# GpSimd adds the exponentials of a head pair in two additions, one for each head

## What is computed

```python
h = _layernorm(x) * (1 + ca) + sa
q, k, v = split(einsum('bse,ehd->bshd', h, w_qkv))        # 16 heads of 64
logits = einsum('bqhd,bkhd->bhqk', q, k) / sqrt(64)        # causal mask
probs = softmax(logits, axis=-1)
x = x + ga * einsum('bshd,hde->bse', einsum('bhqk,bkhd->bqhd', probs, v), w_out)
```

## Time and profile before

| | |
|---|---|
| runs | 2799.43 us median of 3 (2799.24 to 2804.2) |
| profiled execution | 2801.26 us; its span from first to last instruction 2799.5 us |
| TensorE busy | 79% of the span |
| VectorE busy | 58% |
| ScalarE busy | 46% |
| GpSimd busy | 29% (804.5 us) |
| mean granted clock of TensorE | 0.905 of full speed |

### The profile page before, as it was taken

One profiled execution on the slowest core, in us unless ns is written; L12 is line 12 of the kernel. 1 busy time (PEld: TensorE's weight loads), 2 busy tenths in 40 slices (PEclk: granted clock), 3 DMA queues, 4 the chain that ended last, 5 costly groups with the idle time before them and its releaser, 6 DMA issues.

```text
span 2799.5 us, 39653 instructions
## 1 busy us (share of the span) xinstructions
PE 2208.8 (79%) x14753; PEld 898.0 (32%) x14757; DVE 1628.7 (58%) x2829; ACT 1274.6 (46%) x2289; POOL 804.5 (29%) x618
## 2 busy tenths in 40 slices
PE   3989998898777778888767678798868677567776
PEld 2434443444221133444322123344422122121112
DVE  3454456556667456555676735646575865576622
ACT  1433333333357643333357763243326465347762
POOL 1655554343300033443511114344423000001103
PEclk9999999999999898989989998898979898779978
DMA  3000010001110000000210001001110100200000
GB/s 77 15 22 23 15 42 22 12 27 44 39 39 1 1 29 12 22 27 12 64 39 20 12 4 37 12 12 37 38 39 23 46 1 16 84 7 5 5 1 8
DMA packets 81199, 69.14 MB, mean 25 GB/s; under 512 B 46672, under 2 KB 62800, under 8 KB 80496
## 3 DMA queue, kind: packets, MB, share of 16 engines
q1 hardware_dynamic: 81008, 66.60, 8.6%
HBM read 57.58 MB, written 8.98 MB: 24 GB/s over the span
## 4 chain that ended last, share of the span: by engine, by line
PE 62%; DVE 21%; ACT 9%; issue 5%; SPq 2%; DMA 1%; POOL 0%; ACTq 0%; POOLq 0%; DVEq 0%
PE banks L875 60%; DVE pmax L2342 6%; ACT ring L1765 4%; DVE part_max L1943 2%; ACT room L1572 1%; SPq L666 1%; DVE ntmp L1892 1%; PE banks L1014 1%; DVE pick L2083 1%; DVE rstd L1894 1%; DVE room L2092 1%; DVE ntmp L1847 1%; DVE h L1911 1%; DVE stats L1899 1%; DVE oT L1964 1%
## 5 line engine op out<-in xcount | busy, mean ns | idle before, releaser
L816 POOL TENSOR_TENSOR p_sum<-p_sum,ring 128x1024 f32<-128x1024 f32 (+3 forms) x320 | 549.3, 1716 | 806.3 <-PE banks L875 452.4
L2342 DVE TENSOR_REDUCE pmax<-banks 128x2 f32<-128x1024 f32 x512 | 611.1, 1222 | 227.6 <-PE banks L875 225.1
L875 PE MATMUL banks<-ring,v 128*9 128x512 f32 (+4 forms) x2816 | 578.0, 601 | 0.0
L1943 DVE TENSOR_REDUCE part_max<-banks 128x2 f32<-128x1024 f32 (+3 forms) x384 | 365.6, 958 | 335.0 <-PE banks L875 332.4
L875 PE MATMUL banks<-qT,kT 64*128 64x512 f32 (+4 forms) x2048 | 469.8, 522 | 103.1 <-DVE pmax L2342 53.1
L1765 ACT ACTIVATE ring<-banks 128x512 f32<-128x512 f32 x768 | 416.3, 597 | 188.7 <-PE banks L875 187.4
L1524 ACT ACTIVATE ring<-banks 128x1024 f32<-128x1024 f32 (+3 forms) x320 | 245.8, 768 | 472.9 <-PE banks L875 467.8
L875 PE MATMUL banks<-oT 64*128 64x512 bf16 x1024 | 192.3, 414 | 122.5 <-ACT ring L1765 91.8
L875 PEld LDWEIGHTS banks<-qT,kT 64*128 64x128 f32 (+1 forms) x2048 | 146.8, 168 | 379.6 <-issue 120.7
L847 POOL TENSOR_TENSOR room<-room 128x512 f32<-128x512 f32 x32 | 40.6, 1268 | 733.3 <-ACT room L1572 733.3
L875 PE MATMUL banks<-p_sum,v 128*9 128x512 f32 (+1 forms) x768 | 218.4, 646 | 30.2 <-DVE oT L1964 25.2
(11 more groups left out here) (270 smaller groups left out, 2665.9 us busy)
## 6 DMA issues: line engine op xcount, KB each, us to landing
inv_bc<-softmax_inverses SPq DMA_DIRECT2D x64, 256.0 KB, 3.9
w_qk<-in_L_attn_w_qkv SPq DMA_DIRECT2D x64, 64.0 KB, 2.1
low<-in_L_ffn_attention_mask SPq DMA_DIRECT2D x4, 1024.0 KB, 5.8
stage<-rope_constants SPq DMA_DIRECT2D x4, 1024.0 KB, 4.8
x_b<-in_L_attn_x SPq DMA_DIRECT2D x4, 512.0 KB, 4.6
w_v<-in_L_attn_w_qkv SPq DMA_DIRECT2D x32, 64.0 KB, 2.1
stage<-in_L_ffn_w SPq DMA_DIRECT2D x8, 256.0 KB, 6.1
out<-x_b SPq DMA_DIRECT2D x16, 128.0 KB, 1.8
```

The lines of the kernel that those rows point to most:

```text
L816: pool.tensor_tensor(sv, sv, ring0[SLOT[m]][:, :, 0:HALF - lo], ALU.add).then_inc(sem("added"), 1)
L875: return pe.matmul(dst, lhsT, rhs, start=start, stop=stop)
L1943: dve.reduce_max(part_max[:, :, t, c], banks[MAX_PAIR[m]][:, :, 0:w], AX).then_inc(sem("row_max"), 1)
L2342: dve.reduce_max(pmax1[:, :, g, t, c], banks[(0, 3)[USE1[b]["max", m] % 2]][:, :, :], AX).then_inc(sem("row_max1"), 1)
```

## The change

The one addition of both heads becomes two: first the columns of head 0, then those of head 1. A new semaphore `added0` is raised by the first and waited for ahead of the second. The second raises `added`, as the one addition did before; it counts to the same numbers, and all that wait for it stay as they are. The columns, the buffers and the order of all other work are the same.

```diff
-                 lg_sub lg_exp coef halved moe gated x_final
+                 lg_sub lg_exp coef added0 halved moe gated x_final
...
                     sv = p_sum[(2 * n + c) % 3][:, :, lo:]
-                    pool.tensor_tensor(sv, sv, ring0[SLOT[m]][:, :, 0:HALF - lo], ALU.add).then_inc(sem("added"), 1)
+                    pool.tensor_tensor(sv[:, 0, :], sv[:, 0, :], ring0[SLOT[m]][:, 0, 0:HALF - lo], ALU.add).then_inc(sem("added0"), 1)
+                    pool.wait_ge(sem("added0"), NA * n + ADDED[m])
+                    pool.tensor_tensor(sv[:, 1, :], sv[:, 1, :], ring0[SLOT[m]][:, 1, 0:HALF - lo], ALU.add).then_inc(sem("added"), 1)
```

## The result

The changed kernel takes 2764.16 us at the median of four runs (2758.87 to 2778.38) where the kernel before took 2799.34 beside it: ratio 0.9884, 95% interval 0.9842 to 0.9926. A second comparison of the same program gave 2774.29 against 2800.87 us, ratio 0.9900 (0.9876 to 0.9924), and a single further run 2769.06. The median of all nine runs is 2769.1 us. So the change is worth 1.0 to 1.2%, some 27 to 35 us.

A forecast was written before the change was run, and what follows sets the result against it. TensorE, busy 79% of the span, was taken as the bound, with idle waits on VectorE held by GpSimd's additions. Casts +3.5 and port relief -18.4 gave -14.9 us: forecast 2785 us, range 2776 to 2802.

The forecast's parts named there:

- The casts: GpSimd's key casts, queued behind the additions, end 0.25 us later in 14 pairs, delaying TensorE's key weights: +3.5 us.
- The mechanism: A VectorE operation meeting an addition waits only until a half ends, at most 1.27 us, not the whole addition.
- Rival (c): VectorE cannot get in within 0.07 us between halves, so series run as before: 2803.7 us; chance 0.13 with rival (b).
- rival (b): No VectorE series on the chain gains and key casts cost more: 2803.7 to 2810 us; chance 0.13 with rival (c).
- rival (a): VectorE's faster series is swallowed by the next wait, leaving a third to half of gain: 2794 to 2797; chance 0.20.
- GpSimd's queue: Two additions for one add 2.4 us per pair, 77 us over 32 pairs, nearly all within GpSimd's idle time.
- the port's terms: Shorter holds on VectorE cut TensorE's waits by 9.2 us in each of batches three and four, 18.4 us together.
- Picks: Eight VectorE picks and a copy before TensorE's 6.83 us idle: its maximum comes 3.7 us earlier, bounds 2.0 and 4.8.
- Norm: VectorE's norm from 1129 to 1141 us, before a TensorE stall: 1.9 us gained, bounds 1.8 and 3.7.
- The stall before 1241.61: VectorE series before TensorE's row there: 2.9 us earlier at that maximum, 2.0 at the next operation; 2.0 taken.
- Before 1279.41: VectorE series ahead of TensorE's 2.40 us idle there: 1.1 us gained.
- Layer 1's maxima: VectorE's 1.18 us hold by a 512-column addition at 1388.34, before TensorE's wait to 1391.29: 0.5 us gained.

The follow-up runs named there:

- the picks alone: Two additions only in the second pair of the third and fourth batch, one elsewhere, against the kernel before: 2790.42 us, ratio 0.9964.
- the experiment with no wait: The changed kernel without the semaphore wait between the two halves, compared with the kernel before: 2776.41 us, ratio 0.9906.
- the fillers: Kernel before, additions whole, plus 22 unread matrix products in one TensorE wait in each of the third and fourth batches: 2794.61 us, ratio 0.9989.

## Why the prediction missed

**Right.** The casts: 640 additions, a gap of 0.078 us, the weights 0.07 us behind the cast, 0.26 us for each such pair where 0.25 was forecast, less than 2 us more in the first batch. The mechanism: a held pick or Newton step now lasts until the end of a half. The longest Newton step outside the normalisation is 1.19 us; one line of VectorE (ns min/median/max):

```profile
L1894 DVE SCALAR_TENSOR_TENSOR ntmp<-rstd x48: 159/166/1185, 36.8 to 2696.0; 128x8 f32<-128x8 f32 x32, 128x1 f32<-128x1 f32 x16
```

In the first profile of the changed kernel two still take over 1.4 us, a pick 2.42 at 439.92 and a Newton step 2.28 at 491.56, each under a whole normalisation. Rival (c) falls with these rows, rival (b) with the pairs of the first batch, rival (a) with the picks alone, whose 4.2 us stay won, and with the idle sum. The rule of the Trainium skill that I had cited ("SBUF — State Buffer", section "Who interferes with whom"), that the one that starts first keeps the shared pair for its whole instruction, agrees with the rows shown here; the experiment with no wait adds who comes next.

**Smaller misses.** GpSimd's queue grew by 64.8 us of work and 25.1 us of gaps, 90 us where I had 77. And 1.27 us is not the longest addition, as I had said it would be: VectorE holds up some of them in turn. The two longest take 2.13 and 2.14 us, each begun while VectorE works on 1024 columns:

```profile
430.32 2.30 DVE L1849 TENSOR_TENSOR h<-h,mod 128x1024 f32<-128x1024 f32 x1
...
431.61 2.13 POOL L818 TENSOR_TENSOR p_sum<-p_sum,ring 128x512 f32<-128x512 f32 x1
```

**The step that failed is the size of the port's terms.** I took 9.2 us for each late batch and wrote upper bounds that add to 13.0; the third batch lost 12.8 to 13.3 us of idle time, the fourth 9.9 to 10.7 against the first profile of before (the other two have 1.2 and 1.4 us more there). From the rows of the changed kernel:

```profile
1219.17 0.29 PE L877 MATMUL banks<-k_bf,q_bf 64*128 64x128 bf16 x2 [3.71 <-DVE part_max L1945]
...
1256.46 0.63 PE L1016 MATMUL banks<-consts,h 128*128 128x128 f32 x4 [0.78 <-DVE h L1913]
...
1367.80 1.40 PE L877 MATMUL banks<-eye_bf,nmax_hl 128*2 128x128 bf16 x16 [3.49 <-DVE pmax L2344]
```

- Picks: 3.7 taken, 6.83 - 1.99 = 4.84 measured. My walk had the first pick held as before (1.33 us); it came just as a half ended and was free (0.24 at 1065.04).
- Norm: 1.9 taken, 5.87 - 2.12 = 3.75 measured. The walk itself was right: a copy falls under the normalisation (the two from 1125.28 take 2.60 us together), and the next maximum comes only at 1127.80. The mistake was to price the stall by that next maximum. TensorE does not wait for it: it is busy with the 32 products until 1129.4.
- The stall before 1241.61: 2.0 taken, 6.70 - 3.71 = 2.99 measured, for the same reason; I had 2.9 for the maximum that counts.
- Before 1279.41: 1.1 taken, 2.40 - 0.78 = 1.62 measured, 1.3 in the pair.
- Layer 1's maxima: 0.5 taken, and it went the other way, 3.00 to 3.49.

That makes 12.7 us, and it explains the third batch. In the fourth the picks' stall falls by the same 4.84 us (6.83 to 1.99), but the next one, behind another maximum, grows from 1.82 to 2.85 us, so that one microsecond of the relief is swallowed there as rival (a) has it. In the second batch, taken as 0, the stalls themselves stayed within 0.5 us, but 2.6 us went at the start of the layer-1 stage behind it. Net -24.8 us of idle time would have given 2775 us (2800 - 24.8), just under the lower end of my range.

**The term that was left out is TensorE's clock.** I counted idle time alone. The mean of the busy times is 6.2 us lower, which brings it to 2769 us. That a wait of this length costs clock behind it is shown by the fillers; of the lower busy time, 1.8 us in the third pair of the third batch and 0.5 us in that of the fourth go with the shorter wait. The rest differs between executions by more than its mean, up to 9.6 us in a single stage of one program, and I can't assign it to the change. The range should have had it: a term of up to 10 us on either side. The Trainium skill ("TensorE: Matmul & The Clock Gate", section "Part 1: The HAM clock gate") says that how many products run at the lower clock at a kernel's start varies from run to run. Here the like holds in the middle of a kernel: one stage of one program was granted 0.88 in one execution and 0.93 in another.

## What to carry to other kernels

Where one engine holds the port of another, the length of its single instruction matters more than its total: cut it where the held engine's series ends a stall, and keep a wait between the pieces. Price such a stall by the one operation that the waiting engine needs next, not by the one behind it. Cut only where there is a series to relieve and room in the queue (quarters in the late batches alone gave 2751 us; everywhere, 2766), and give a shortened wait of TensorE a second term, from nothing to the whole difference, for the products behind it.

## What the runs showed of the hardware

- Between two GpSimd instructions that stand back to back with no semaphore wait, one waiting VectorE operation goes through; with a wait of 0.08 us two do, the second in its free time of 0.28 us. With whole, half and quarter pieces of 1024 columns a held pick takes 2.42, 1.36 and 0.81 us.
- A one-column copy on GpSimd takes 0.19 us and opens the port as well as a long instruction's end.
- After 5.87 us of idleness 32 products took 5.65 us in the third batch and 5.98 in the fourth, with fillers 3.84 in both; after 2.12 us of idleness 3.84 in the third and 5.47 in the fourth. The granted clock from the wait's end to the last product was 0.65 before and 1.00 with fillers.
- Two executions of one program differed by 9.6 us in the busy time of one stage that the edited instructions don't touch, at granted clocks of 0.88 and 0.93.
